# One more wait before the gathers of a routed expert layer: each pair of row gathers waits until the pair before it has landed

## What is computed

```python
x = x + attn(layernorm(x))     # 16 heads of 8, 4 key/value heads, window of 32 tokens, rotary
h = layernorm(x)
logits = h @ router_w.T        # 8 experts
w, sel = top2(logits)          # two experts per token, gates with a jitter threshold
for e in range(8):
    t = silu(h @ w_gate[e].T) * (h @ w_up[e].T)      # 128 -> 256
    out += dense_w[:, e:e+1] * (t @ w_down[e].T)     # 256 -> 128
x = x + out
```

## Time and profile before

| | us |
|---|---|
| median of 3 timed runs | 562.23 |
| lowest and highest | 561.99, 567.3 |
| span of the profiled execution | 673.3 |

### The profile page before, as it was taken

How to read it: one execution, slowest core, us unless ns; L and a number is a source line. 1 busy time by engine, 2 the same in 40 slices (tenths; PEclk the granted TensorE clock), 3 DMA queues, 4 the chain that set the end, 5 groups by cost and what they waited for, 6 DMA issues and landing times.

```text
span 673.3 us, 23426 instructions
## 1 busy us (share of the span) xinstructions
PE 550.8 (82%) x7519; PEld 473.6 (70%) x7519; DVE 424.6 (63%) x1700; ACT 370.5 (55%) x1170; POOL 345.8 (51%) x536
## 2 busy tenths in 40 slices
PE   3899999999999999987657669888887878887860
PEld 1578887777878777875537569777787778776850
DVE  5788898898989988883554226355444454544452
ACT  4467776666757766651246437455554555554530
POOL 3333346667776666763343381435455444556355
PEclk9999999999999999995756779899899899999895
DMA  7333333233332222222111223334444443443333
GB/s 215 67 72 74 71 81 96 65 82 82 69 72 46 53 45 53 53 48 62 33 54 44 65 67 96 99 114 135 115 120 126 111 123 102 126 122 107 103 107 82
DMA packets 126310, 58.20 MB, mean 86 GB/s; under 512 B 54000, under 2 KB 121712, under 8 KB 126192
## 3 DMA queue, kind: packets, MB, share of 16 engines
q1 hardware_dynamic: 117424, 39.03, 23.3%
q0 software_dynamic: 8192, 16.79, 8.6%
q10 hardware_dynamic: 576, 0.88, 0.4%
HBM read 28.15 MB, written 24.58 MB: 78 GB/s over the span
## 4 chain that ended last, share of the span: by engine, by line
PE 69%; another core or an unknown queue 9%; issue 8%; ACT 5%; DMA 3%; DVE 2%; POOL 2%; SPq 1%; ACTq 1%; POOLq 0%; DVEq 0%
PE chb L727 16%; PE pv L581 7%; PE chb L639 6%; PE pm L592 5%; PE pp L752 5%; PE pp L661 5%; PE pv L752 4%; PE chb L630 4%; PE chb L626 3%; PE tp L744 2%; PE tp L684 2%; POOL ga L1368 2%; PE tp L554 2%; PE tp L560 2%
## 5 line engine op out<-in xcount | busy, mean ns | idle before, releaser
L1368 POOL DMA_INDIRECT ga<-expert_out,row_all x128 | 122.3, 955 | 137.1 <-DVE yb L1257 83.9
L1297 POOL DMA_INDIRECT expert_in<-xn,slot_r x128 | 126.9, 992 | 121.5 <-DVE slot_r L921 96.5
L727 PE MATMUL chb<-xbT,wcur 128*128 128x128 f32 x1144 | 162.4, 288 | 0.0
L727 PEld LDWEIGHTS chb<-xbT,wcur 128*128 128x128 f32 x1144 | 150.6, 205 | 0.0
L1250 DVE TENSOR_TENSOR hT<-sil,chb 128x256 f32<-128x256 f32 x143 | 60.1, 420 | 114.2 <-ACT sil L507 86.3
L507 ACT ACTIVATE sil<-chb 128x256 f32<-128x256 f32 x143 | 54.9, 384 | 124.2 <-PE chb L727 57.2
L417 ACT ACTIVATE pT<-chb 128x512 f32<-128x512 f32 x128 | 77.1, 602 | 69.8 <-PE chb L639 59.5
L938 DVE TENSOR_REDUCE mx<-chb 128x8 f32<-128x512 f32 x128 | 86.7, 685 | 18.0 <-PE chb L639 13.9
L524 ACT COPY wcur<-wgu 128x512 f32 x143 | 89.9, 629 | 5.6 <-issue 5.3
L744 PE MATMUL tp<-ident,xb 128*128 128x128 f32 x143 | 42.5, 297 | 48.9 <-issue 38.6
L581 PEld LDWEIGHTS pv<-vext,pT 128*64 128x64 f32 x1984 | 68.1, 140 | 13.8 <-issue 13.3
(11 more groups left out here) (140 smaller groups left out, 1051.1 us busy)
## 6 DMA issues: line engine op xcount, KB each, us to landing
xb<-expert_in SPq DMA_DIRECT2D x143, 64.0 KB
expert_out<-yb SPq DMA_DIRECT2D x71, 128.0 KB
xa<-x SPq DMA_DIRECT2D x16, 256.0 KB
out<-oo SPq DMA_DIRECT2D x31, 128.0 KB
qk<-qk SPq DMA_DIRECT2D x64, 48.0 KB
wgu<-w_gu SPq DMA_DIRECT2D x16, 128.0 KB
expert_in<-xn,slot_r POOLq DMA_INDIRECT x128
ga<-expert_out,row_all POOLq DMA_INDIRECT x128
```

Source lines behind the costliest of these rows:

```text
L727: last = nc.tensor.matmul(chb[:, b % 4, n * P:(n + 1) * P], wcur[:, b % 3, n * P:(n + 1) * P], xbT[:, b % 4, :], start=True, stop=True)
L1297: nc.gpsimd.indirect_dma_start(xs_dram, bass.IndirectOffsetOnAxis(ap=slot_r[:, q % 4, 2 * v + k:2 * v + k + 1], axis=0), xn2[:, t % 16, :] ...
L1368: nc.gpsimd.indirect_dma_start(ga[:, q % 2 * TPS + v, j, :], None, ys_dram[0:min(blocks, LIVE) * P, :], bass.IndirectOffsetOnAxis(ap=row_a ...
```

## The change

Before the two gathers of tile k, for k from 1 to 55 (sequences 0 to 13), GpSimd also waits until both gathers of tile k-1 have landed. The semaphore is the one on which `combine(k-1)` waits. The gathers of tile 0 and those of tiles 56 to 63 have no new wait. Nothing else is changed: order, buffers and the other waits are the same.

```diff
                     wait(pool, comb_ok, (q - 1) * TPS)
                     for v in range(TPS):
+                        k = q * TPS + v
                         if q < SEQS - 2 and (v or part == 0):
                             pool.wait_ge(yb_ok, 2 * TPS * (q + 1) + 2 * (SLACK + 1) + 2 * v + 1)
+                        if 0 < k < (SEQS - 2) * TPS:
+                            pool.wait_ge(gath[(k - 1) % (2 * TPS)], ((k - 1) // (2 * TPS) + 1) * 32)
                         for j in range(2):
                             nc.gpsimd.indirect_dma_start(
```

## The result

| | before | after |
|---|---|---|
| median of 4 timed runs, us | 563.11 | 657.74 |
| lowest and highest | 561.99, 567.3 | 655.68, 665.26 |
| ratio, with its 95% interval | | 1.1694 (1.1621 to 1.1766) |
| span of the profiled execution | 673.3 | 657.4 |

The change costs 94.6 us. The direction is the one forecast; the size is nearly three times the 31.8 us forecast, and 657.7 us lies above all of the range given (561 to 612).

A forecast was written before the change was run, and what follows sets the result against it. GpSimd's gathers, each pair waiting for the last landing, were to become the bound: 237.1 us from the copy of block 24 on against 204.6 before, +32.5, so about 594 us, range 561 to 612.

The forecast's parts named there:

- C: Time from pair to pair of gathers on GpSimd under the new wait: 1.26 + 2.5 = 3.75 us, bounds 3.15 and 3.85.
- tail: Kernel before, from the copy of block 135 to the end: about 28.7 us in the profile, taken as 27.
- first sign: In the profile after, pairs in a row would stand 3.7 to 3.8 us apart if the prediction was right.
- they cost nothing in themselves: The 55 added wait instructions on GpSimd were priced at nothing, since GpSimd waits at each pair anyway.
- the waking of the waiting engine, which GpSimd pays as well: The 2.5 us from second gather to VectorE's `acc` was said to include waking, and was used for GpSimd too.
- T: Time per block in the timed kernel before, from block 24 on: taken as 1.6 us, between 1.45 and 1.72.
- The lead: Gathers run ten blocks ahead of `combine`, 12 us usable; losing 0.55 us a pair, used up after some 22 pairs.
- The dismissal of the profile's stalls: Most stalls in the profiled block loop, at 2.04 us a block, were held absent from the timed runs.
- The profile's span should move little: The profiled execution after would take 418.4 + 237.1 = 655.5 us against 673.3, moving little, within some 8 us.
- Hidden anyway: Rival: two blocks take as long as C, so the waits pass unnoticed; 562 us, chance 0.14.
- Less crowding: Rival: fewer gathers in flight slow the blocks less, winning back 8 us; 554 us, chance 0.06.
- Tail alone: Rival: the lead nearly lasts and only the last paced pairs push the 16 gathers behind them; 567 to 581 us, chance 0.20.

The follow-up runs named there:

- e_again: The kernel before, unchanged, profiled and timed again: 563.3 us, with a profiled span of 560.8 us.
- e_each: Against the changed kernel, the second gather of each pair also waits until the first has landed: 751.8 us.
- e_order: Against the kernel before, an always fulfilled wait for a landing four pairs back is put first, making the wait for copy `yb` a separate instruction: 564.5 us.
- e_swap: Against the changed kernel, the wait for the landing is put ahead of the wait for the copy `yb`: 639.4 us.
- e_last8: Against the changed kernel, the new wait is kept for tiles 48 to 55 only: 576.1 us.
- e_first: Against the changed kernel, the landing wait stands first in every pair's list of waits, also at a sequence's first tile: 638.2 us.
- e_dist2: Against the changed kernel, each pair waits for the pair before the preceding one (k-2, k from 2 to 55): 563.25 us.

## Why the prediction was right in sign and wrong in size

The working can be checked term by term, since the prediction's sum starts at the copy of block 24, which comes at 362.8 us in after and 363.6 in e_again.

| term | forecast | measured |
|---|---|---|
| after: copy of block 24 to the first gather | 1.1 | 1.1 |
| after: 54 intervals of C | 202.5 | 259.9 |
| after: the interval with `rows(1)` | 6.85 | 6.85 |
| after: last paced pair, 15 gaps, last gather to the end | 26.6 | 26.7 |
| **after, together** | **237.1** | **294.6** |
| before: 111 blocks | 177.6 | 167.2 |
| before: tail | 27 | 30.0 |
| **before, together** | **204.6** | **197.2** |
| **difference** | **+32.5** | **+97.4** |

Less the 0.8 us by which block 24 came earlier, that is the 96.6 us between the two spans, and 94.6 between the medians.

**The step that failed: C, the time from pair to pair.** The prediction took 3.75 us with bounds of 3.15 and 3.85; the 54 plain intervals have a mean of 4.81. That is 259.9 - 202.5 = 57.4 us, all of the miss of 64.9 but 7.5. It comes in three parts. The prediction's own first sign, pairs 3.7 to 3.8 us apart, did not appear.

- 0.71 us a pair, 38 us in all, are the time between the wait's being fulfilled and the gather behind it. The prediction had said of the new waits that "they cost nothing in themselves" and that the 2.5 us include "the waking of the waiting engine, which GpSimd pays as well". It had read that waking from VectorE's rows, whose combine needs no separate wait. The runs showed that GpSimd pays more than VectorE. e_each shows both forms in one kernel, e_order shows it without a DMA as the releaser, and e_swap gets 18 us back by the order alone. Not all of the 0.71 can be saved that way: the carried form still takes 0.24.
- (4.59 - 3.75 - 0.71) x 54 = 7 us are the landing itself, 2.6 us as the median instead of 2.5. The bound of 3.85 had allowed for 0.1.
- (4.81 - 4.59) x 54 = 12 us are late landings. The group of the 112 gathers has them:

```profile
L1371 POOL DMA_INDIRECT ga<-expert_out,row_all x112: 940/951/1059, 363.9 to 631.9; - x112
```

The view of that line gives 2.4, 2.6 and 4.4 us as the least, median and longest time from issue to landing. A kernel in which each landing lets go the next one adds up every late one; in the kernel before they vanish in a lead of 12 us. The prediction's C was one typical landing, used as if it were the mean.

**The smaller step: the base it was set against.** T was taken as 1.6 us and is 1.506: -10.4 us. Its upper bound of 1.72 came from a block 24 copied at 344 us at the earliest, where e_again has 363.6; with that figure the same sum allows 1.54. The tail was cut from 28.7 to 27 for a pause taken as the profile's own, and is 30.0: +3.0. Together the kernel before had 7.4 us less to hide the gathers than assumed, which adds to the loss.

**The lead went sooner, for the same two reasons.** A pair fell behind by 4.59 - 3.01 = 1.6 us and not by 0.55. From the second gather of a pair to VectorE's use of it the trace has 12.3 us for tile 0, 7.9 for tile 5 and 2.6 for tile 10; the prediction had 22 pairs. In e_again it is 12.3, 17.3 and 12.3 for the same tiles, and 12.1 at tile 45.

**What held.** The mechanism did: GpSimd's chain of landings is the bound, waits of GpSimd name its own gathers, VectorE waits for rows long before the end, and TensorE stands behind it. The chain's other terms were right to 0.1 us, `rows(1)` among them, where the landing hides under the 3.7 us of arithmetic. The dismissal of the profile's stalls held too. "The profile's span should move little" came out true (657.4 against a forecast of 655.5) for no good reason: the sum of 418.4 + 237.1 joins a block 24 that came 56 us late in the disturbed execution with a chain that was forecast 57 us too short.

**The rivals.** "Hidden anyway" would have needed C below 3.2; it is 4.81. "Less crowding" has little to win back: the blocks of e_again have 1.45 us beside the gathers, outside of one stretch that one pair in flight does not shorten either. "Tail alone" is e_last8, 576 us, a part of the loss and not its whole.

The Trainium skill, DMA: Bandwidth & Descriptors, section on the anatomy of one DMA on the gpsimd path, gives the formula by which the prediction estimated 2.15 us for 64 KB and 3.41 us for a pair; the trace has 2.5 to 2.6 us from issue to the waiting engine. The remark in its section on latency and other measured facts, that lighter HBM load makes the fixed cost smaller, would matter little here: in after the median is 2.60 us beside the blocks and 2.53 in the tail, where no block's rows are loaded.

**What stays open.** Why some landings take up to 4.4 us. In after they fall together with a load of 16 KB of instructions on queue q8, as in the window 473 to 478 us, which holds one gather:

```profile
q8 instruction: 1, 0.02, 1.8%
...
ga<-expert_out,row_all POOLq DMA_INDIRECT x1, 4.4
```

From the first gather to tile 55 there are 15 such loads. Nine of them begin between a pair's second gather and its landing, and these are the nine pairs, beside that of `rows(1)`, where it takes over 4 us from the second gather to the next pair. The other six begin outside, and their pairs have 3.2 to 3.4 us. The nine exceed the median of 3.33 by 11 us in all, nearly the whole of the 12 us above. e_first shows the same: its ten slowest pairs, 3.7 to 5.5 us, all have a load there. That is a close coincidence in time and no proof, for no run took the loads away. Open, too, are why the common landing is 0.1 us longer in e_first than in e_swap, and why the gathers of the profiled e_swap began 7 us later than those of after.

No version here beats the kernel before: its own tail is 16 gathers issued at 1.25 us each, which none of these edits shortens.

## What to carry to other kernels

A wait for a transfer's landing ahead of the next transfer turns an engine's issue rate into a latency. Price the whole round, from release to the next issue on the engine that waits, at its mean with the late landings in it, and not by one landing read on another engine. Where such a wait must be, put the one that comes last first in the list, so that the transfer carries it, and wait on an older transfer if the buffers allow it: one pair further back, the same wait was free (e_dist2).

## What the runs showed of the hardware

- A gather on GpSimd starts about 0.71 us after its release where the releasing wait is a separate instruction (0.72 after VectorE's start on the same landing in after, 0.75 after the end of a copy in e_order), and 0.24 to 0.28 us where the gather carries the wait (e_swap, e_again). That the gather carries the first wait is inferred from these rows and the instruction counts.
- From a gather's start to the start of an engine that waits for it, 64 KB in 128 rows take 2.5 to 2.6 us as a rule, and up to 4.4. In after each landing that was more than 0.6 us late had an instruction load on q8 beside it; the cause is open. In after 11 of the 55 pair intervals are over 5 us, one of them that of `rows(1)`.
- Two gathers without a wait between them start 1.25 to 1.26 us apart, 0.95 of it the instruction, in the loop and in the tail, in before and after alike.
